# Attention stage: the normalized rows transposed block by block, and the table, residual and row transfers issued at another place of the step

## The reference

```python
x = x + attn_a(layernorm(x))        # one row of v, broadcast
x = x + ffn(layernorm(x))
x = x + attn_b(layernorm(x))        # the stage of the change
x = x + ffn(layernorm(x))

# attn_b: 16 heads of 64, blocks of W = 128 rows, each block sees itself and the block before it
q, k, v = rope(h @ Wq.T + bq), rope(h @ Wk.T + bk), h @ Wv.T + bv
scores = qb @ kcat.T / 8            # 128 x 256, band mask
ctx = softmax(scores) @ vcat
out = merged(ctx) @ Wo.T + bo
```

## Time and profile before

| | |
|---|---|
| median of 3 runs | 1627.08 us (1626.82 to 1629.59) |
| the profiled execution | 1629.63 us, of which the span (first to last instruction) is 1627.8 us |
| TensorE, VectorE, ScalarE, GpSimd busy | 92%, 86%, 81%, 70% |
| mean granted TensorE clock | 0.979 of 2.4 GHz |
| attention stage | from about 205 us to 1440 us, 64 steps of about 18.4 us |

### The profile page before, as it was taken

One profiled execution on the slowest core, in us unless ns is written; L12 is line 12 of the kernel. 1 busy time (PEld: TensorE's weight loads), 2 busy tenths in 40 slices (PEclk: granted clock), 3 DMA queues, 4 the chain that ended last, 5 costly groups with the idle time before them and its releaser, 6 DMA issues. The chain is left out here.

```text
span 1627.8 us, 46830 instructions
## 1 busy us (share of the span) xinstructions
PE 1503.2 (92%) x16866; PEld 1145.2 (70%) x16866; DVE 1403.6 (86%) x3859; ACT 1324.8 (81%) x2442; POOL 1137.7 (70%) x911
## 2 busy tenths in 40 slices
PE   5999878899999999999999999999999999869998
PEld 4888745576767676666767676767676767658887
DVE  5999668899989999999999898999898889857885
ACT  5999658888878888888888787888788878749996
POOL 4665367778777887878788777787787777623443
PEclk7999989999999999999999999999999999979999
DMA  5242247889998999999998999899989998962331
GB/s 210 92 124 99 65 100 128 169 164 176 169 183 159 176 161 184 165 187 170 170 184 157 172 166 169 168 176 172 173 151 175 165 166 159 172 157 69 109 111 70
DMA packets 728445, 247.92 MB, mean 152 GB/s; under 512 B 688148, under 2 KB 715032, under 8 KB 728216
## 3 DMA queue, kind: packets, MB, share of 16 engines
q1 hardware_dynamic: 727512, 244.53, 78.1%
q10 hardware_dynamic: 704, 0.40, 0.1%
HBM read 47.73 MB, written 25.17 MB: 45 GB/s over the span
## 5 line engine op out<-in xcount | busy, mean ns | idle before, releaser
L1283 DVE CUSTOM_DVE_ANT_0 at_prob<-banks,at_masks,pre_s_scale 128x256 f32<-128x256 f32 (+1 forms) x1024 | 421.3, 472 | 25.8 <-PE banks L1697 9.3
L1446 ACT ACTIVATE at_prob<-at_prob,at_top 128x256 f32<-128x256 f32 (+1 forms) x1024 | 428.3, 490 | 16.5 <-DVE at_top L1283 14.1
L1295 DVE TENSOR_TENSOR at_halves<-at_prob,at_halves 128x1024 f16<-128x1024 f32 (+1 forms) x256 | 331.7, 1296 | 3.1 <-ACT at_halves L1455 3.1
L1582 PE MATMUL banks<-at_xt,pre_w_h 128*128 128x512 f16 x1024 | 299.4, 385 | 12.4 <-ACT at_v_l L1474 7.6
L1697 PE MATMUL banks<-at_kt,at_qt 32*128 32x256 f32 (+1 forms) x4096 | 253.4, 384 | 31.5 <-issue 20.8
L1455 ACT ACTIVATE at_halves<-at_prob 128x1024 f16<-128x1024 f32 (+1 forms) x256 | 263.4, 1029 | 6.1
L1697 PEld LDWEIGHTS banks<-at_kt,at_qt 32*128 32x128 f32 x4096 | 198.6, 187 | 93.1 <-issue 88.4
L1653 PE MATMUL banks<-at_v_h,at_pt 128*128 128x65 f16 x1984 | 208.9, 195 | 32.7 <-DMA at_pt<-at_halves 25.8
L1653 PEld LDWEIGHTS banks<-at_v_h,at_pt 128*128 128x128 f16 x1984 | 182.1, 98 | 73.2 <-DMA at_pt<-at_halves 41.0
L1175 POOL TENSOR_TENSOR at_kt<-at_k_by 128x512 f32<-128x512 f32 x128 | 171.5, 1340 | 77.3 <-DVE at_halves L1295 65.6
L1165 POOL TENSOR_TENSOR at_q_by<-at_q_first,at_tables 128x512 f32<-128x512 f32 x128 | 175.5, 1375 | 61.5 <-DVE at_halves L1295 60.8
(11 more groups left out here) (123 smaller groups left out, 3319.1 us busy)
## 6 DMA issues: line engine op xcount, KB each, us to landing
f_x<-in_x SPq DMA_DIRECT2D x16, 512.0 KB, 3.7
x_after_ffn<-f_x SPq DMA_DIRECT2D x16, 512.0 KB, 2.7
at_x_res<-x_after_ffn SPq DMA_DIRECT2D x64, 128.0 KB, 3.1
x_after_attention<-at_x_res SPq DMA_DIRECT2D x64, 128.0 KB, 2.7
f_x<-x_after_attention SPq DMA_DIRECT2D x16, 512.0 KB, 4.4
out_x<-f_x SPq DMA_DIRECT2D x16, 512.0 KB, 3.0
at_x_ln<-x_after_ffn SPq DMA_DIRECT2D x32, 128.0 KB, 3.2
at_tables<-in_cos SPq DMA_DIRECT2D x16, 256.0 KB, 4.0
```

Of the source, the lines that this page charges most:

```text
L1283: last = nc.vector.tensor_tensor_reduce(out=prob[:, n % 2, h, low:2 * P], in0=s_ps[:, h, n % 2 * 2 * P + low:(n % 2 + 1) * 2 * P], in1=mas ...
L1295: nc.vector.tensor_tensor(parts[:, 1, :, :], prob[:, n % 2, :, keys_from(t, b):2 * P], parts[:, 0, :, :], ALU.subtract).then_inc(p_low, 1)
L1446: last = nc.scalar.activation(at, at, ACT.Exp, bias=top[:, n % 2, h:h + 1], scale=-1.0)
L1582: last = nc.tensor.matmul(pr_ps[:, half, :].rearrange("p (b t) -> p b t", b=SB), w[wp][:, k, at:at + P], xt[:, r, xp, :, k, :], start=n == ...
```

## The change

1. `x_halves` and `xt` are laid out by block first. SyncE transposes one block per step (`turn_x(n)` with n = t + 7) instead of four blocks at g = 0. Only the first super-block is still transposed at once (`first_turn_x`, at t = -4).
2. `turn_x(n)` waits for `x_low` of its block, for the transposition before it, and for `v_done[1]` >= NG (S - 1), where S is now the super-block of block n, so (t + 7) // 4.
3. In SyncE's list of a step, `turn_x`, `load_residual` (now one step earlier, t - 3), `store`, `load_x` and the tables stand behind `turn_p(t, 2)`. Before, the transposition of x and the tables, the residual and the store stood ahead of `turn_p(t, 1)`.
4. The cosine table is loaded at g = 3 for S + 2, the sine table at g = 1 for S + 1.

```diff
-        def turn_x(S):
-            if big(S):
-                sp.wait_ge(x_low, SB * (S + 1))
+        def turn_x(n):
+            if step(n):
+                S, blk = divmod(n, SB)
+                sp.wait_ge(x_low, n + 1)
+                sp.wait_ge(xt_in[(n - 1) // SB % 2], xt_turned(n - 1))
                 need(v_done[1], NG * (S - 1))
...
-                sp.dma_start(xt[:, S % 2, :, :, :, :].rearrange("p e b k t -> p (e b k) t"),
-                             x_halves[:, :, :, :].rearrange("p e b c -> p (e b c)"),
+                sp.dma_start(xt[:, S % 2, blk, :, :, :].rearrange("p e k t -> p (e k) t"),
+                             x_halves[:, blk, :, :].rearrange("p e c -> p (e c)"),
                              transpose=True).then_inc(xt_in[S % 2], 16)
...
         def at_step(t):
             S, g = divmod(t, NG)
             turn_p(t - 1, 3)
-            if g == 0:
-                turn_x(S + 1)
+            if t == -4:
+                first_turn_x()
             turn_context(t - 2)
             turn_p(t, 0)
-            load_residual(t - 4)
-            store(t - 6)
-            if g == 0 and S >= 0:
-                load_tables(S + 1)
             turn_p(t, 1)
             turn_p(t, 2)
+            if t + 7 >= SB:
+                turn_x(t + 7)
+            load_residual(t - 3)
+            store(t - 6)
             if t == -8:
                 load_x(SB)
             load_x(t + 13)
+            if g == 3 and S >= -1:
+                load_table(S + 2, 0)
+            if g == 1 and S >= 0:
+                load_table(S + 1, 1)
...
@@ scalar: x_high_of(n) @@
-                need(xt_in[(S - 1) % 2], xt_ready(S - 1))
+                if S > 0:
+                    act.wait_ge(xt_in[(S - 1) % 2], xt_turned(n - SB))
```

More of the change, by code:

```diff
@@ L914, in attention_stage @@
     eps = sb("eps", [P, SB])
-    x_halves = sb("x_halves", [P, 2, SB, C], F16)
-    xt = sb("xt", [P, 2, 2, SB, CK, P], F16)
+    x_halves = sb("x_halves", [P, SB, 2, C], F16)
+    xt = sb("xt", [P, 2, SB, 2, CK, P], F16)
     x_res = sb("x_res", [P, RB, C])
@@ L999, in turned, with xt_turned @@
         return 16 * (n // 2 + 1)
+    def xt_turned(n):
+        S, blk = divmod(n, SB)
+        return 16 * (SB * (S // 2) + blk + 1) if S % 2 else 16 * (1 + SB * (S // 2 - 1) + blk + 1) if S else 16
     def xt_ready(S):
-        return 16 * (S // 2 + 1)
+        return xt_turned(SB * S + SB - 1)
     def tab_ready(S):
@@ L1071, in turn_context, with first_turn_x @@
                              transpose=True).then_inc(ct_in, 16)
-        def turn_x(S):
-            if big(S):
-                sp.wait_ge(x_low, SB * (S + 1))
+        def first_turn_x():
+            sp.wait_ge(x_low, SB)
+            sp.wait_ge(past.moved[0], past.stores(2 * past.SLOTS))
+            sp.dma_start(xt[:, 0, :, :, :, :].rearrange("p b e k t -> p (b e k) t"),
+                         x_halves[:, :, :, :].rearrange("p b e c -> p (b e c)"),
+                         transpose=True).then_inc(xt_in[0], 16)
+        def turn_x(n):
+            if step(n):
+                S, blk = divmod(n, SB)
+                sp.wait_ge(x_low, n + 1)
+                sp.wait_ge(xt_in[(n - 1) // SB % 2], xt_turned(n - 1))
                 need(v_done[1], NG * (S - 1))
-                if S < 2:
-                    sp.wait_ge(past.moved[S], past.stores(S + 2 * past.SLOTS))
-                sp.dma_start(xt[:, S % 2, :, :, :, :].rearrange("p e b k t -> p (e b k) t"),
-                             x_halves[:, :, :, :].rearrange("p e b c -> p (e b c)"),
+                if n == SB:
+                    sp.wait_ge(past.moved[1], past.stores(1 + 2 * past.SLOTS))
+                sp.dma_start(xt[:, S % 2, blk, :, :, :].rearrange("p e k t -> p (e k) t"),
+                             x_halves[:, blk, :, :].rearrange("p e c -> p (e c)"),
                              transpose=True).then_inc(xt_in[S % 2], 16)
@@ L1093, in load_x, with load_table @@
                 sp.dma_start(x_ln[S % 2][:, blk, :], x_in[:, n, :]).then_inc(ln_in[blk], 16)
-        def load_tables(S):
+        def load_table(S, e):
             if big(S):
@@ L1101, in load_tables @@
                 at = SB * P * (S % SPB)
-                for e, table in enumerate((cos, sin)):
-                    sp.dma_start(tables[:, S % 2, e, :], table[:, at:at + SB * P]).then_inc(tab_in[S % 2], 16)
+                sp.dma_start(tables[:, S % 2, e, :], (cos, sin)[e][:, at:at + SB * P]).then_inc(tab_in[S % 2], 16)
         def load_residual(i):
@@ L1122, in opening @@
                 load_x(n)
-            load_tables(0)
+            load_table(0, 0)
+            load_table(0, 1)
             sp.dma_start(bv_cols[:, :], bv).then_inc(const_in, 16)
@@ L1201, in x_low_of @@
                 pool.wait_ge(x_high, n + 1)
-                nc.gpsimd.tensor_tensor(x_halves[:, 1, blk, :], x_ln[S % 2][:, blk, :], x_halves[:, 0, blk, :],
+                nc.gpsimd.tensor_tensor(x_halves[:, blk, 1, :], x_ln[S % 2][:, blk, :], x_halves[:, blk, 0, :],
                                         ALU.subtract).then_inc(x_low, 1)
@@ L1336, in x_low_of @@
                 dve.wait_ge(x_high, n + 1)
-                nc.vector.tensor_tensor(x_halves[:, 1, blk, :], x_ln[S % 2][:, blk, :], x_halves[:, 0, blk, :],
+                nc.vector.tensor_tensor(x_halves[:, blk, 1, :], x_ln[S % 2][:, blk, :], x_halves[:, blk, 0, :],
                                         ALU.subtract).then_inc(x_low, 1)
@@ L1599, in values @@
                             last = nc.tensor.matmul(
-                                pr_ps[:, half, blk * 2 * P:(blk + 1) * 2 * P], xt[:, r, xp, 2 * half + blk, k, :],
+                                pr_ps[:, half, blk * 2 * P:(blk + 1) * 2 * P], xt[:, r, 2 * half + blk, xp, k, :],
                                 w[wp][:, k, VC + g * 2 * P:VC + (g + 1) * 2 * P],
```

4 lines of the change are left out of this document (2 added, 2 removed).

## The result

| | us |
|---|---|
| before, median | 1627.32 (1626.82 to 1629.59) |
| after, median | 1761.67 (1756.93 to 1764.08) |
| ratio after / before | 1.0819, 95% interval 1.0793 to 1.0846 |
| forecast | 1739 (1690 to 1810) |
| spans of the profiled executions | 1627.8 and 1755.1, so +127.3 |

The medians lie 134.4 us apart and the profiled executions, from which all rows are read, 127.3 us: the one of after is the fastest of its four.

What follows compares the result with a forecast made beforehand. It took TensorE as the bound, except in steps g = 0, where transfers end last. 1629.6 - 38 + 10 + 140 = 1742 us, less 2.5 us for the median: 1739 us, range 1690 to 1810 us.

Steps and rivals of the forecast that it cites:

- Part 3: SyncE's turn_x at g = 1 waits for values, holding back turn_p(t, 3): 14 x 10 = 140 us.
- Part 1: Transposition of x leaves g = 0, no longer delaying turn_p(t, 0): 38 us gain, at least 20 us.
- The row with 14.50 us of GpSimd in 20.60: Last g = 0 step shown: long despite little GpSimd work, so the whole excess was booked as gain.
- Part 2: A quarter in every step behind turn_p(t, 2) crowds transfers ahead of turn_p(t + 1, 0): 10 us more.
- The low-clock rival: TensorE stays at 1.2 GHz another 3 us after each pause: 14 x 3 = 42 us, 1781 us, chance 0.17.
- Made up again: Idle 0.45 us of each of the next three steps recovers 19 us of the pauses: 1720 us, chance 0.10.
- The fast rival: SyncE reaches turn_x only after the values end, so its wait costs nothing: 1599 us, chance 0.04.

Runs made afterwards that it cites:

- e1: The changed kernel with one number altered: SyncE transposes block t + 6 in step t instead of t + 7; 1615.31 us.
- e3: The changed kernel with turn_x(t + 7) moved to the end of SyncE's list of a step; 1718.07 us.
- e12: The changed kernel with turn_x(t + 7) moved behind turn_p(t, 3) in the next step's list, ahead of the context; 1705.12 us.
- e9: e2 without GpSimd's inverse_std for the super-blocks S >= 2 and VectorE's waits for it; 1600.44 us.
- e2: e1 with load_residual, store and both tables back in their old place, behind turn_p(t, 0) and at g = 0; 1607.88 us.
- e10: e2 with inverse_std moved, within GpSimd's step g = 0, between key_product(t + 1, 3) and the wait for p_low; 1607.46 us.

## Why the prediction was right, point by point

- **Part 3, the wait (forecast 14 x 10 = 140 us).** Right in place, count and size: 14 x 10.5 = 147 us. Its steps, as medians over the 14 places of the timelines of after, from the release of turn_x on: turn_p(t, 3) issued at 3.5 us (forecast 3.15), its product at 8.7 us (7.75), turn_p(t + 1, 0) issued at 8.8 us, its product at 14.4 us (13.8). TensorE's idle times before the first product are 7.1 to 9.4 us (7 to 8), SyncE's waits 11.8 us (some 10). The quarter took 1.19 us to issue on the empty queue, not 0.8, and turn_p(t, 3) landed after 5.1 us, not 4.6, behind four transfers; these are most of the difference. e1 shows it by removal, e3 and e12 by moving what stands behind it.
- **Part 1, g = 0 (forecast -38 us).** Mis-sized. The steps fell from 21.0 to 19.5 us, 14 x 1.5 = 21 us, and not to the 18.4 to 18.9 us that I had named. The row with 14.50 us of GpSimd in 20.60 misled me: it shows that the transposition alone is enough to lengthen a step, not that nothing else stands right behind it. When the one delay went, the other, inverse_std and the collisions that follow, was next late (e9). The step that misled me is t = 56, the one of the 14 without an inverse_std, since no super-block is left to prepare. In it the whole excess did go: it lasts 18.41 us in after (first row below). The bound of 20 us had it.
- **Part 2, the crowd behind turn_p(t, 2) (forecast +10 us).** About right, for a reason partly wrong. In after the steps with g = 3 grew by 0.24 us, 3 us in all; e1 against e2 prices the moved transfers at 7 us. The quarter's issue is not on the line through the two sizes of `pt`: its median is 1.63 us in the full queue, its least 1.19 (the half-size piece has 1.23), so SyncE issues 6.5 us for what one of 2.8 us did, not 3.2. I had drawn that line through the least of one size and the median of the other. The 3.7 us more per super-block are hidden in e2, whose steps g = 1 to 3 last 18.3 to 18.4 us.
- **The sum.** -38 + 10 + 140 = 112 forecast, -21 + 3 + 147 = 129 measured in the steps, 127.3 between the spans. The missing 17 us are part 1; parts 2 and 3 are 7 us off each, one down and one up, and cancel. The median moved by 134 us, 7 more than the profiled execution.
- **The low-clock rival (0.17, 1781 us).** It didn't come. The clock did fall to 0.50, 2.2 to 5.4 us behind the end of the values, and in 13 of the 14 places it was back at 1.00 after 11.2 to 13.8 us, before the second product started. The forecast itself had 0.65 us a place for it (13.8 against 13.15), close to the estimated 0.5 us. In e12, where work was ready while the clock was low, it cost 1.2 us a place.
- **Made up again (0.10, 1720 us).** Nothing was: the steps with g = 3 behind the pause last 18.6 us, not less than the 18.3 of the kernel before, and those with g = 0 as long as in e1, which has no pause.
- **The fast rival (0.04).** Fell; the order is fixed by the lists, as argued.

The step t = 56 of after in the windows, and the issue times of the quarter by tile in after, beside the earlier trace rows:

```profile
1417.71:1436.12 18.41, 17.95 (x240) 13.38 (x240) 16.81 (x51) 15.12 (x29) 14.40 (x11) 1.00 1.01 175
...
L1094 SPq DMA_TRANSPOSE at_xt<-at_x_halves x60: 1188/1629/1952, 202.2 to 1430.9; - x60
```

## What to carry to other kernels

When work is moved ahead by less than a buffer's period, write down for each piece which reader of the slot it must wait for and in which step of the reader's list that is: here one block of four came one step too early, and shifting the index by one turned 8.2% slower into 0.7% faster. The price of a wait in an in-order queue is not the wait's own length (11.8 us) but what the bounding engine wants next from behind it; it can be worked out from issue and landing times before anything is built (10 forecast and 10.5 measured here), with the clock behind the pause counted where work is ready (e12 came out 1.9 us above its forecast). And where one delay is taken away, look for the next one right behind it before booking the whole of it as a gain.

## What the runs showed of the hardware

A transposing DMA has a floor of about 1.2 us of issue on SyncE: the least is 1.19 us for a piece of 128 x 512 values, 1.23 us for 128 x 1024 and 1.63 us for one of 128 x 2048 (all in after). Plain transfers issued just ahead of a transposition lengthen its issue, from 1.90 to 3.07 us in the medians of the 14 places of e3 and after. GpSimd's operation on four elements took 1.19 instead of 0.20 us beside VectorE's subtraction of two SBUF tensors (e10, before). TensorE's granted clock fell from 1.00 to 0.50 in each of the 14 pauses of after, when TensorE had been idle for 2.2 to 5.4 us, and rose again with TensorE at work, in 13 of them before the second product. What the low clock costs depends on whether work is ready: 1.2 us a place in e12, an estimated 0.5 us in after, where most of it ran beside a transfer that TensorE had to wait for.
